# Last feed-forward group of the second network over six PSUM banks, with the output written group by group

## The reference

```python
x = x + L0_xattn(layernorm(x), ctx, ctx)   # cross attention, 16 heads
x = x + L0_ffn(layernorm(x))               # 6 layers: local attention + gated feed-forward
x = x + L1_xattn(layernorm(x), ctx)        # two-way attention with a gate
x = x + L1_ffn(layernorm(x))               # 2 layers: local attention + gated feed-forward
...
# the feed-forward of one layer of the last stage:
h = shift_token(x)
h = (h - h.mean(-1)) / sqrt(h.var(-1) + 1e-5) * lg + lb
a, g = split(h @ w1 + b1)                  # 341 columns each
x = x + (a * gelu(g)) @ w2 + b2
```

## Time and profile before

| what | us |
|---|---|
| median of 3 runs | 2380.1 |
| the profiled execution | 2380.36 |
| its span, first to last instruction | 2378.5 |
| PE busy | 2165.0 |
| DVE busy | 1744.3 |
| ACT busy | 1706.8 |
| POOL busy | 1338.4 |
| mean granted clock of PE | 0.961 of full |

### The profile page before, as it was taken

One profiled execution on the slowest core, in us unless ns is written; L12 is line 12 of the kernel. 1 busy time (PEld: TensorE's weight loads), 2 busy tenths in 40 slices (PEclk: granted clock), 3 DMA queues, 4 the chain that ended last, 5 costly groups with the idle time before them and its releaser, 6 DMA issues.

```text
span 2378.5 us, 88152 instructions
## 1 busy us (share of the span) xinstructions
PE 2165.0 (91%) x33770; PEld 1468.6 (62%) x33770; DVE 1744.3 (73%) x4834; ACT 1706.8 (72%) x5904; POOL 1338.4 (56%) x1270
## 2 busy tenths in 40 slices
PE   6988999999999999999999999999997787999996
PEld 4655666666666666666666666666665374666652
DVE  3868877778777777877777778777773376788853
ACT  3746878887787788877878787787885154787861
POOL 1317766666666666666666666665662035666640
PEclk8988999999999999999999999999998797999996
DMA  4001221112211221122211212112211100000000
GB/s 107 2 4 30 72 55 45 40 49 64 57 40 43 65 55 47 42 52 59 58 44 43 60 49 57 41 41 53 53 45 33 28 1 12 13 15 15 15 6 22
DMA packets 141470, 96.92 MB, mean 41 GB/s; under 512 B 61784, under 2 KB 132992, under 8 KB 141056
## 3 DMA queue, kind: packets, MB, share of 16 engines
q1 hardware_dynamic: 141056, 91.28, 15.1%
HBM read 23.11 MB, written 1.05 MB: 10 GB/s over the span
## 4 chain that ended last, share of the span: by engine, by line
PE 78%; issue 7%; ACT 7%; DVE 6%; POOL 2%; SPq 0%; DMA 0%; POOLq 0%; ACTq 0%; DVEq 0%
PE bank L643 22%; PE bank L754 8%; PE bank L664 7%; PE bank L721 6%; PE bank L698 5%; PE bank L808 4%; PE bank L790 4%; PE bank L799 3%; PE bank L707 3%; PE bank L692 2%; PE bank L585 2%; ACT arena L1273 1%; PE bank L593 1%; PE bank L606 1%; ACT L1273 1%
## 5 line engine op out<-in xcount | busy, mean ns | idle before, releaser
L643 PE MATMUL bank<-wqkv,hs 128*128 128x512 f32 x1344 | 675.4, 621 | 31.8 <-ACT arena L1251 15.2
L1486 POOL TENSOR_TENSOR arena<-arena,rnorm 128x512 f32<-128x512 f32 x448 | 454.4, 1043 | 381.3 <-DVE rnorm L1722 380.1
L1479 POOL TENSOR_TENSOR arena<-arena 128x512 f32<-128x512 f32 x448 | 567.0, 1273 | 167.8 <-DVE arena L1673 167.5
L1220 ACT ACTIVATE arena<-bank,amx 128x64 f32<-128x64 f32 x1536 | 457.5, 334 | 7.1 <-DVE amx L1737 6.7
L1668 DVE TENSOR_TENSOR arena<-bank,rot 128x512 f32<-128x512 f32 x448 | 306.6, 684 | 89.5 <-PE bank L643 85.8
L643 PEld LDWEIGHTS bank<-wqkv,hs 128*128 128x128 f32 x1344 | 230.8, 193 | 220.6 <-issue 161.2
L1197 ACT ACTIVATE arena<-bank 128x512 f32<-128x512 f32 x448 | 263.9, 616 | 125.8 <-PE bank L664 124.8
L1220 ACT ACTIVATION_READ_ACCUMULATOR arena<-bank,amx 128x1 f32 x1536 | 350.8, 228 | 0.0
L1673 DVE TENSOR_TENSOR arena<-bank,rot 128x256 f32<-128x256 f32 x896 | 333.1, 413 | 0.0
L1191 ACT ACTIVATE arena<-bank 128x512 f32<-128x512 f32 x448 | 264.7, 644 | 71.9 <-DVE arena L1673 71.6
L664 PEld LDWEIGHTS bank<-ident,arena 128*128 128x128 f32 x1792 | 213.2, 142 | 156.1 <-issue 125.4
(11 more groups left out here) (170 smaller groups left out, 3223.1 us busy)
## 6 DMA issues: line engine op xcount, KB each, us to landing
arena<-arena SPq DMA_DIRECT2D x768, 64.0 KB
wqkv<-in_L_ffn_Wqkv_dram SPq DMA_DIRECT2D x24, 256.0 KB
hs<-z SPq DMA_DIRECT2D x128, 32.0 KB, 1.8
fx<-z SPq DMA_DIRECT2D x32, 128.0 KB, 2.2
hs<-z SPq DMA_DIRECT2D x128, 31.8 KB, 1.9
fx<-z SPq DMA_DIRECT2D x32, 127.0 KB, 2.5
wqkv<-in_L_ffn_Wqkv_dram SPq DMA_DIRECT2D x24, 128.0 KB
w<-in_L_ffn_W_dram SPq DMA_DIRECT2D x6, 341.0 KB
```

The lines of the kernel that those rows point to most:

```text
L643: nc.tensor.matmul(bank[o][:], src[:], wqkv[w][:, off:off + 512], start=True, stop=True).then_inc(AT[name] if part < 2 else AT[name][i], 1)
L1220: ins = nc.scalar.activation(pb[i][0][p % 2][:, h * DH:(h + 1) * DH], bank[3 + g][:, j * DH:(j + 1) * DH], ACT.Exp, bias=amx[p % 2][:, i, ...
L1479: nc.gpsimd.tensor_tensor(t, t, rs[i][c], ALU.add).then_inc(AT["ak" if c else "aq"][i], 1)
L1486: nc.gpsimd.tensor_tensor(t, t, rnorm[p % 2][:, i, HU * c:HU * c + HU].unsqueeze(2).to_broadcast([P, HU, DH]), ALU.mult).then_inc(AT["mk" ...
```

## The change

Seven things are done to the last stage, most of them only for the last group (`f == LAST`, that is 31).

1. Its three gate products go to banks 3, 4 and 5 and its three up products to banks 6, 7 and 2, and none of them waits for a bank. The DVE copies of its gate products are gone; Gelu reads the bank.
2. Its down product goes to bank 1, and its three matmuls wait for their own third of `hid`. For every other group too the wait on `hid` now stands ahead of each of the three matmuls, with the same value as before.
3. The residual of a group, `outer(k)`, is done by DVE after steps 111, 113 and 115, and at the end for the last group.
4. The transposes of a group, `turn_back(k)`, are done by PE after steps 112, 113 and 115 and at the end, into bank 0 or 1.
5. The copies from the bank, `output(k)`, are done by ACT at the same places, into four slots of their own.
6. SP issues four transfers of 256 KB, each when its copy is done.
7. The loops end after step 117 instead of 119; the two steps left out are empty.

```diff
@@ sync @@
-            sp.wait_ge(io_dve, 2 * NBLK)
-            sp.dma_start(out.rearrange("b t d -> t b d"), cen.rearrange("p (b d) -> p b d", b=NB)).then_inc(out_st, 16)
-            sp.wait_ge(out_st, 16)
+            for k in range(NBLK):
+                sp.wait_ge(in_act, NBLK + k + 1)
+                sp.dma_start(out[4 * k:4 * k + 4].rearrange("b t d -> t b d"), quads(o_st[k])).then_inc(out_st, 16)
+            sp.wait_ge(out_st, 16 * NBLK)
@@ tensor @@
+            def turn_back(k):
+
+                pe.wait_ge(FF["outer"], NBLK + k + 1)
+                at(pe, in_act, NBLK + k - 1)
+                if k < 2:
+                    pe.wait_ge(AT["sqk" if k else "sqq"], un(1, 111))
+                for j in range(4):
+                    b = 4 * k + j
+                    mm = nc.tensor.transpose(bank4[k % 2][:, j, :], base_x[:, b * P:(b + 1) * P], ident[:])
+                mm.then_inc(io_ps, 1)
...
-                    normal_free(s)
                     if f % 4 == 0 and c == 0:
                         pe.wait_ge(ld_ff, 192 * (f // 4 + 1))
                     pe.wait_ge(FF["aff"], f + 1)
-                    at(pe, FF["ge"], 3 * f + c)
-                    nc.tensor.matmul(bank[2][0:w, :], w1[f // 4 % 2][:, HID + o:HID + o + w], fxn, start=True, stop=True
+                    if f < LAST:
+                        normal_free(s)
+                        at(pe, FF["ge"], 3 * f + c)
+                    nc.tensor.matmul(bank[2 if f < LAST else GATE[c]][0:w, :], w1[f // 4 % 2][:, HID + o:HID + o + w], fxn, start=True, stop=True
...
-                    pe.wait_ge(FF["hid"], 3 * f + 3)
                     at(pe, FF["cen"], min(f + 2, 4 * (ph["layer0"] + ph["depth"])))
+                    if f == LAST:
+                        pe.wait_ge(in_act, NBLK + 2)
                     for c in range(3):
                         w = CH[c][1]
-                        mm = nc.tensor.matmul(bank[2][:], w2[f // 4 % 2][0:w, c, :], hid[c][0:w, :],
+                        pe.wait_ge(FF["hid"], 3 * f + (c + 1 if f == LAST else 3))
+                        mm = nc.tensor.matmul(bank[2 if f < LAST else 1][:], w2[f // 4 % 2][0:w, c, :], hid[c][0:w, :],
...
+                        if s in (112, 113, 115):
+                            turn_back(min(s - 112, 2))
...
-            pe.wait_ge(FF["outer"], 2 * NBLK)
-            for k in range(NBLK):
-                for j in range(4):
-                    b = 4 * k + j
-                    mm = nc.tensor.transpose(bank4[k][:, j, :], base_x[:, b * P:(b + 1) * P], ident[:])
-                mm.then_inc(io_ps, 1)
+            turn_back(3)
@@ scalar @@
+            def output(k):
+
+                act.wait_ge(io_ps, 2 * NBLK + k + 1)
+                nc.scalar.activation(o_st[k], bank[k % 2][:], ACT.Copy).then_inc(in_act, 1)
...
-                        act.wait_ge(FF["ge"], 3 * f + c + 1)
-                        nc.scalar.activation(gl[c][0:w, :], gl[c][0:w, :], ACT.Gelu, bias=b1[f // 4 % 2][0:w, 3 + c:4 + c]
+                        if f < LAST:
+                            act.wait_ge(FF["ge"], 3 * f + c + 1)
+                        else:
+                            act.wait_ge(FF["up"], 6 * f + c + 1)
+                        nc.scalar.activation(gl[c][0:w, :], gl[c][0:w, :] if f < LAST else bank[GATE[c]][0:w, :], ACT.Gelu, bias=b1[f // 4 % 2][0:w, 3 + c:4 + c]
...
+                        if s in (112, 113, 115):
+                            output(min(s - 112, 2))
@@ vector @@
+            def outer(ph, k):
+
+                dve.wait_ge(FF["z"], 4 * (ph["layer0"] + ph["depth"] - 1) + k + 1)
+                b = slice(k * BLK, (k + 1) * BLK)
+                nc.vector.tensor_tensor(base_x[:, b], base_x[:, b], z[:, b], ALU.add).then_inc(FF["outer"], 1)
...
+                    if f == LAST:
+                        return
...
+                        if s in (111, 113, 115):
+                            outer(ph, (s - 111) // 2)
...
-            for k in range(NBLK):
-                dve.wait_ge(io_ps, 2 * NBLK + k + 1)
-                nc.vector.tensor_copy(cen[:, k * BLK:(k + 1) * BLK], bank[k][:]).then_inc(io_dve, 1)
+            outer(PHASES[1], 3)
```

More of the change, by code:

```diff
@@ L30 @@
 NLAYER = 8
+LAST = 4 * NLAYER - 1
+GATE, UP = (3, 4, 5), (6, 7, 2)
 def rotary_constants(window):
@@ L109, in build @@
         ctx_t = sb("ctx_t", [P, TOK])
-        arena = sb("arena", [P, 47 * BLK])
+        arena = sb("arena", [P, 49 * BLK])
         big = arena[:, 0:8 * TOK]
@@ L127, in build @@
         y_d, y_e, y_m = slot(8)[:, 0:256], slot(9)[:, 0:256], slot(10)[:, 0:256]
+        o_st = [slot(45 + k) for k in range(NBLK)]
         heads = lambda a: a.rearrange("p (h d) -> p h d", h=HU)
@@ L794, in ff_up @@
                     o, w = CH[c]
[L795 to L799, removed]
+                    if f < LAST:
+                        normal_free(s)
+                        if c == 0:
+                            pe.wait_ge(FF["ge"], 3 * f + 3)
+                        at(pe, FF["hid"], 3 * f + c)
+                    nc.tensor.matmul(bank[2 if f < LAST else UP[c]][0:w, :], w1[f // 4 % 2][:, o:o + w], fxn, start=True, stop=True
                                      ).then_inc(FF["up"], 1)
@@ L1024, in step_1 @@
                         probs(0, s - 1, 0)
-                for s in range(lo, hi + 8):
+                for s in range(lo, hi + (8 if ni == 0 else 6)):
                     if ni == 0:
@@ L1430, in _ @@
             act_phase(PHASES[1])
+            output(3)
         @block.gpsimd
@@ L1799, in ff_hidden @@
                     dve.wait_ge(FF["gelu"], 3 * f + c + 1)
-                    nc.vector.scalar_tensor_tensor(out=hid[c][0:w, :], in0=bank[2][0:w, :], scalar=b1[f // 4 % 2][0:w, c:c + 1],
+                    nc.vector.scalar_tensor_tensor(out=hid[c][0:w, :], in0=bank[2 if f < LAST else UP[c]][0:w, :], scalar=b1[f // 4 % 2][0:w, c:c + 1],
                                                    in1=gl[c][0:w, :], op0=ALU.add, op1=ALU.mult).then_inc(FF["hid"], 1)
@@ L1805, in ff_close @@
                     dve.wait_ge(FF["y"], f + 1)
-                    nc.vector.scalar_tensor_tensor(out=z[:, b], in0=bank[2][:], scalar=lnp[f // 4 % 2][:, 2:3], in1=z[:, b],
+                    nc.vector.scalar_tensor_tensor(out=z[:, b], in0=bank[2 if f < LAST else 1][:], scalar=lnp[f // 4 % 2][:, 2:3], in1=z[:, b],
                                                    op0=ALU.add, op1=ALU.add).then_inc(FF["z"], 1)
@@ L1930, in dve_phase @@
                         step_1(s)
-                layers = 4 * (ph["layer0"] + ph["depth"])
-                dve.wait_ge(FF["z"], layers)
-                for k in range(NBLK):
-                    b = slice(k * BLK, (k + 1) * BLK)
-                    nc.vector.tensor_tensor(base_x[:, b], base_x[:, b], z[:, b], ALU.add).then_inc(FF["outer"], 1)
+                        if s in (111, 113, 115):
+                            outer(ph, (s - 111) // 2)
+                for k in range(NBLK if ni == 0 else 0):
+                    outer(ph, k)
             dve.wait_ge(X0["res"], NB)
```

## The result

The changed kernel takes 2356.5 us, the median of 7 runs (2354.75 to 2365.61), beside 2380.1 of the kernel before, also 7 runs. The ratio is 0.9915, with a 95% interval of 0.9900 to 0.9929: 20.2 us less, between 16.9 and 23.8. (The two medians lie 23.6 apart; the ratio and its interval are taken over all the runs, and I go by them.) The profiled execution took 2356.19 us, its span 2354.4, which is 24.1 under the 2378.5 of before.

A forecast was written before the change was run, and what follows sets the result against it. PE was 91% busy, but the last 38 us were taken as bound by a chain of waits at half clock. 19.8 us saved less 2.75 paid, net -17.0 from 2380.36, gave 2363.3 us, range 2356 to 2371.

The forecast's parts named there:

- Products and clock: Last group on PE: six products without bank waits save 6.3 us; clock rising 5 us into the run saves 5.7.
- The rival of the clock staying at half: Last group's PE run: granted clock stays 0.50, so only 10.9 us net is saved, 2369.5 us; chance 0.14.
- Residuals, transposes, copies: Kernel's end: one group's work left instead of four; residuals save 1.9 us, transposes and copies 3.1.
- The transfer: Last output transfer: a quarter of the data left, landing 2.3 us after issue instead of 5.1, saving 2.8 us.
- What is paid: Steps 111 to 114: output work moved forward delays the chain by 0.6, 1.7 and 0.45 us, 2.75 in all.
- The queue behind ACT's wait: End of step 112: in-order ACT waits for the first transposes, then copies, so the next projection starts 1.7 us later.
- The rival of further stalls: Steps 112 and 113: delayed work meets later waits, 3 to 5 us more, 2367 to 2368 us; chance 0.10.
- The added waits: Down products of the 31 other groups: extra waits ahead of matmuls are hidden, cost 0; unhidden up to 14.9 us.
- The rival on the transposes: Last group's run: transposes do not count as work for the clock, losing 1.3 us, 2364.6 us; chance 0.06.
- The slower case: New PE gap at 2301.4 in steps 112 to 114 costs the clock, making the kernel 2383.7 us; chance 0.03.

The follow-up runs named there:

- banks only: Changed kernel with its end undone: six banks kept, but four residuals, sixteen transposes, four copies and one transfer at the end; ratio to before 0.9944.
- copies later: Changed kernel with ACT's copies of the first two output groups moved behind the second outputs of steps 113 and 114; ratio to before 0.9916.
- one transfer: Changed kernel with one 1 MB transfer at the end instead of four; one run, no ratio; first last-stage projection to span end 387.0 us against 384.1.
- one wait: Changed kernel with a single wait on `hid` ahead of the down product of the 31 other groups, as before; 2361.1 us, ratio to before 0.9926.
- before, filled: Kernel before, with unread matmuls put into PE's idle time in steps 114 to 116, also between the last group's products; ratio to before 0.9955.
- end only: Changed kernel with its banks undone: the last group uses bank 2 alone, the output still goes group by group; ratio to before 0.9966.
- filled, products: Changed kernel with matmuls that nobody reads put into PE's idle time in steps 114 and 115; ratio to before 0.9909.
- filled, transposes: Changed kernel with transposes that nobody reads, as long as filler matmuls, put into PE's idle time in steps 114 and 115; ratio to before 0.9906.

## Why the prediction was right

2363.3 us was forecast, 17.0 under the profiled execution of before; 20.2 were measured, and the interval of 16.9 to 23.8 takes in 17.0 only at its lower edge. The median, 2356.5, lies 6.8 under the forecast and just inside the range, whose low end was 2356. That it did not fall outside is in part luck: six later runs of the same kernel, "changed again", have a median of 2360.7, and the part ahead of the last stage, which the change does not touch, moves a trace by several us. So I judge the mechanism by the steps, against the table of stretches:

- *Products and clock.* 6.3 + 5.7 = 12.0 forecast, 12.7 in the trace. The run without gaps is there, and the clock came back in it. I had it rise after 5 us; it was 3.6 here, and 3.0 to 5.2 in the six traces that have such a run (changed twice, banks only, copies later, one transfer, one wait). The rival of the clock staying at half is out. The experiments also say how the sum divides: the clock is a term of its own, and is had without the banks. In "before, filled" the clock alone took 11.6 us off B, because a clock held from the mean on speeds up the whole chain of the last group, not only the end of a run.
- *Residuals, transposes, copies.* 1.9 + 3.1 = 5.0 forecast, 4.9 measured, with PE at full clock as assumed.
- *The transfer.* 2.8 forecast, 2.8 measured, landing after 2.3 us; "one transfer" puts the 2.8 back. The estimate by the Trainium skill, "DMA: Bandwidth & Descriptors", section "Anatomy of one DMA", was 4.4 us for the large one, 2.6 for the small one and 1.8 between them; 5.1, 2.3 and 2.8 were measured. That section gives its figures for transfers that GpSimd issues, and these are issued by SP.
- *What is paid.* 2.75 forecast, 2.3 measured. The parts by the starts in the timelines: `outer(0)` 0.5 of 0.6, `output(0)` 1.5 of 1.7, `output(1)` 0.5 of 0.45; some 0.2 of this is made good before the mean of group 31. The queue behind ACT's wait was the largest, as said, and "copies later" shows its cause. The rival of further stalls is out for this trace; in the four with the fall in step 112 and the copies where the change puts them, A is 3.8 to 4.0 over before.
- *The added waits.* No cost shows, as forecast.

What the sum did not have is the down product of group 30. In the trace of before it ran at half clock, 5.30 us on PE from 2329.99 on, and I carried that over; in the changed kernel it took 2.81 (both from the timeline of PE; the earlier trace rows has the same product of group 31 at half clock, 5.47). With the mean ahead of it this is the -3.0 between the mean and the first gate product. The prediction named it only as a reason for the low end of the range, 2.6 us. 17.0 and 3.0 make 20.0, against 20.2; the closeness says little, with an interval that reaches over 3 us either way.

It is not shown that these 3.0 us are an effect of the change. The down product of group 30 ran at full clock in all five traces that have both halves of the change and no fillers, and at or near half clock in before, "banks only" and "end only". But the banks come only after it, and "end only" and "one wait" have the same matmuls on PE up to there, with the same idle time ahead of each of the last ones. One had the clock at half and the other at full (end only first; L782 is the mean of group 31):

```profile
2331.46 1.06 PE L815 MATMUL bank<-arena,w 128*85 128x512 f32 x2 [0.94 <-DVE arena L1825]
2333.41 2.03 PE L782 MATMUL bank<-fx,mean_w 128*128 128x512 f32 x2 [0.89 <-DVE arena L1825]
2336.27 4.79 PE L824 MATMUL bank<-arena,w 128*128 128x512 f32 x6 [0.83 <-issue]
```

```profile
2336.22 1.06 PE L817 MATMUL bank<-arena,w 128*85 128x512 f32 x2 [0.94 <-DVE arena L1835]
2338.16 1.10 PE L782 MATMUL bank<-fx,mean_w 128*128 128x512 f32 x2 [0.89 <-DVE arena L1835]
2340.09 2.81 PE L829 MATMUL bank<-arena,w 128*128 128x512 f32 x6 [0.83 <-issue]
```

The granted clock fell at 2333.4 in the first, as the mean began, and at 2344.8 in the second, 6.7 us after the start of the mean. So here, too, one program can have either level, and how often each comes is not known from one trace of a kernel.

The rival on the transposes is also out, twice: banks without transposes and with them saw the clock return after 3.0 and 3.6 us, and fillers made of transposes held it. The slower case was not seen. A fall of the clock in step 112 was, for 3.4 us in six traces, but at a gap that the kernel before has too, not at the new one. It cost 1.4 to 1.7 us, and dense work followed at once.

## What to carry to other kernels

At the end of a pipeline, where other work no longer fills the gaps, each hand-over from one engine to the next is paid twice: once as idle time, and once more because the idle time takes TensorE's clock, which makes the work between slower too. Ask both what an extra bank saves in hand-overs and whether PE stays busy enough to keep the clock; fillers that compute nothing brought half of this change by themselves. And when work is moved forward onto an engine that runs in order, place it behind the instruction that another engine waits for: the copy in front of `outputs` cost 1.3 us for nothing. And where one program can run at either level of the clock, a single trace of each kernel shows one outcome: compare traces that had the same one, or take several.

## What the runs showed of the hardware that I had not expected

- The same idle time can be followed by either level of the clock. The wait of 2.0 us ahead of L680 in step 112 was followed by 0.50 in six traces and by 1.00 in seven, among them the changed kernel with 1.00 and "one wait", "filled, products" and "filled, transposes" with 0.50, whose programs are one up to there but for the place of a wait.
- Between the down product and the last sixteen transposes 3.25 us of idle time were followed by 3.24 us of transposes in "banks only", with the clock at 0.50 from about 2351.2; in "before, filled" the same sixteen took 1.97 us after 3.38 us of idle time, at full speed:

```profile
2352.22 1.97 PE L1153 MATMUL bank<-ident,base_x 128*128 128x128 f32 x16 [3.38 <-DVE base_x L1954]
```

- The time ahead of the last stage, one program in all kernels, differed by up to 11.5 us between traces (1968.6 to 1980.1), half a per cent of the whole. It starts in the first network: its first projection begins between 174.7 and 176.5 in all of them.
